# Two attentions and a 64-expert feed forward on one core: down projection four pairs behind the up projection, and a new table of side work

## The reference

```python
shared = silu(xf @ Ws_up) @ Ws_down
aff = xf @ centroids.T
_, idx = top_k(aff + expert_biases, 8)
w = sigmoid(take_along_axis(aff, idx)); w = w / (w.sum() + 1e-8)
cw = zeros((T, 64)).at[arange(T)[:, None], idx].add(w)
h = silu(einsum('td,edf->etf', xf, W_up))
y = einsum('etf,efd->etd', h, W_down)
return shared + einsum('etd,te->td', y, cw)
x = x + attn_a(layernorm(x)); x = x + ffn(layernorm(x))
x = x + attn_b(layernorm(x)); x = x + ffn(layernorm(x))
```

## Time and profile before

| | us |
|---|---|
| median of 3 runs | 1095.35 (1095.05 to 1095.57) |
| the profiled execution | 1094.11 |
| its span in the trace | 1092.0 |
| PE busy | 1001.1 (92%) |
| DVE busy | 956.8 (88%) |
| ACT busy | 890.1 (82%) |
| POOL busy | 487.9 (45%) |

### The profile page before, as it was taken

The page is one execution under the profiler, slowest core; times in us unless marked ns, Lnnn a source line. Parts: engine busy times, 40 slices in busy tenths (PEclk is TensorE's granted clock), DMA queues, the critical chain, the costliest instruction groups (busy, mean ns, idle before and its releaser), DMA issues.

```text
span 1092.0 us, 21659 instructions
## 1 busy us (share of the span) xinstructions
PE 1001.1 (92%) x8016; PEld 513.8 (47%) x8016; DVE 956.8 (88%) x1186; ACT 890.1 (82%) x1466; POOL 487.9 (45%) x893
## 2 busy tenths in 40 slices
PE   6389999999999999999999999999899899999998
PEld 3022222222222222222232337777777777777876
DVE  7799999999999999999999948787877987687665
ACT  5179999999999999999999986777776776677775
POOL 3363545454545555554456466433224332432431
PEclk9579999999999999999999999999999999999999
DMA  8911110111011101110110017665577476757773
GB/s 278 303 33 46 52 50 4 50 51 51 3 51 51 51 4 51 51 34 20 51 51 22 2 27 192 152 163 135 143 175 176 134 172 167 192 145 176 187 192 101
DMA packets 80472, 108.90 MB, mean 100 GB/s; under 512 B 23536, under 2 KB 33520, under 8 KB 80368
## 3 DMA queue, kind: packets, MB, share of 16 engines
q1 hardware_dynamic: 66336, 100.98, 35.1%
q10 hardware_dynamic: 14032, 6.55, 2.3%
HBM read 95.57 MB, written 11.93 MB: 98 GB/s over the span
## 4 chain that ended last, share of the span: by engine, by line
DVE 51%; PE 29%; ACT 7%; issue 5%; DMA 4%; POOL 2%; ACTq 1%; SPq 1%; DVEq 0%; POOLq 0%
DVE NEGMAX L1060 43%; PE PS L1451 8%; PE PS L1453 7%; PE PS L1452 7%; DVE HL L1109 2%; PE PS L1353 2%; ACT HH L943 2%; DVE HF L1101 2%; ACT PR L855 2%; DMA RAWU<-in_L_ffn_W_up_dram 2%; PE PS L1326 1%; PE PS L1232 1%; ACT L950 1%; POOL WUL L627 1%; DMA GATE<-gate_d 1%
## 5 line engine op out<-in xcount | busy, mean ns | idle before, releaser
L1060 DVE TENSOR_REDUCE NEGMAX<-PS 128x1 f32<-128x1024 f32 x512 | 584.5, 1208 | 9.9 <-PE PS L1289 9.2
L855 ACT ACTIVATE PR<-PS 128x512 f32<-128x512 f32 x1024 | 538.7, 600 | 36.5 <-PE PS L1326 24.2
L1353 PE MATMUL PS<-PR,VG 128*32 128x256 f32 (+1 forms) x3840 | 321.2, 406 | 17.5 <-ACT PR L855 2.0
L1326 PE MATMUL PS<-QB,KB 32*128 32x512 bf16 x1024 | 260.1, 387 | 3.0 <-DMA QB<-shift_d 1.7
L1289 PE MATMUL PS<-KA,QA 32*128 32x512 bf16 x1024 | 204.4, 397 | 30.9 <-DVE NEGMAX L1060 22.5
L1101 DVE TENSOR_TENSOR HF<-PS,GATE 128x1024 f32<-128x1024 f32 x128 | 156.2, 1221 | 73.8 <-ACT PS L950 72.0
L950 ACT ACTIVATE PS<-PS 128x1024 f32<-128x1024 f32 x128 | 129.3, 1010 | 93.5 <-PE PS L1453 93.1
L1326 PEld LDWEIGHTS PS<-QB,KB 32*128 32x128 bf16 x1024 | 75.0, 91 | 239.2 <-ACT PR L855 138.1
L943 ACT ACTIVATE HH<-HF 128x1024 fp32r<-128x1024 f32 (+1 forms) x136 | 139.7, 1028 | 19.5 <-DVE HF L1101 18.7
L1109 DVE TENSOR_TENSOR HL<-HF,HH 128x1024 fp32r<-128x1024 f32 (+1 forms) x104 | 129.8, 1248 | 12.5 <-ACT HH L943 12.5
L767 POOL TENSOR_TENSOR HL<-HF,HH 128x1024 fp32r<-128x1024 f32 (+1 forms) x32 | 70.2, 2194 | 155.0 <-ACT HH L943 155.0
(11 more groups left out here) (186 smaller groups left out, 970.6 us busy)
## 6 DMA issues: line engine op xcount, KB each, us to landing
GATE<-gate_d SPq DMA_DIRECT2D x256, 256.0 KB, 4.1
QA<-q_stack SPq DMA_DIRECT2D x64, 128.0 KB, 2.6
QB<-q_stack SPq DMA_DIRECT2D x16, 256.0 KB, 3.0
KB<-k_stack SPq DMA_DIRECT2D x16, 256.0 KB, 3.0
KA<-k_stack SPq DMA_DIRECT2D x60, 64.0 KB, 2.4
q_stack<-PARTS SPq DMA_DIRECT2D x12, 256.0 KB, 4.3
k_stack<-PARTS SPq DMA_DIRECT2D x12, 256.0 KB, 4.4
RAWU<-in_L_ffn_W_up_dram ACTq DMA_DIRECT2D x4, 512.0 KB, 11.9
```

Of the source, the lines that this page charges most:

```text
L855: nc.scalar.activation(PR[:, s % PRING, r, :], PS[:, SCORE_BANK[n], :], ACT.Exp, scale=SCALE_A).then_inc(p_ready, 1)
L1060: nc.vector.tensor_reduce(NEGMAX[:, hs % 2, col:col + 1], PS[:, e:e + 2, :].rearrange("p b n -> p (b n)"), axis=AX_X, op=ALU.max, negate=T ...
L1326: mm(PS[:, SCORE_BANK[n], :], KB[strip, u, mt * P:(mt + 1) * P], QB[strip, u, half * BANK:(half + 1) * BANK], start=True, stop=True).then_ ...
L1353: last = mm(PS[STRIP * r:STRIP * (r + 1), 7, cols], VG[:, u, mt, r // 2, :], PR[:, s % PRING, r, cols], start=mt == 0, stop=mt == TB - 1 a ...
```

## The change

- `LAG` goes from 3 to 4: `down` runs four pairs behind `up`. HH and HL have five places; HF keeps four, under a number of its own (`FPLACES`).
- ACT copies AFF out at the beginning of the step of its `affinity`, with the other side work, and no longer behind silu and `high`. The sigmoid alone stays at the step's end.
- `CWT`, `GRAM`, `GK` and `VMIX` have one copy, not two; POOL's `sum` waits for the `gate_T` before it, and the sigmoid waits for the `sum` before it.
- The table is written anew from chunk 2 on. Routing of chunk 3 moves from (2, 1), (2, 3), (2, 5), (2, 7) to (2, 4), (2, 6), (2, 7), (2, 8) for `affinity`, `top`, `sum`, `gate_T`. That of chunk 5 moves from (3, 16), (4, 1), (4, 3), (4, 5) to (3, 14), (3, 16), (4, 1), (4, 3), and that of chunk 7 likewise in chunks 5 and 6. The second attention's items in chunks 2 and 4 come one step later, up to `mix_back` at (3, 3) and (5, 3). `out_b` stays at (3, 5), (3, 6), (5, 5) and (5, 6).
- 32 `low` stay on POOL; (2, 8), (3, 3), (4, 8) and (5, 3) go to DVE, (1, 16), (2, 2), (4, 2) and (6, 2) come to POOL.

```diff
-LAG = 3
+LAG = 4
+FPLACES = 4
 HPLACES = LAG + 1
...
-    (2, 0): [("x_T", ("f", 3))], (2, 1): [("affinity", 3)], (2, 3): [("top", 3)], (2, 5): [("sum", 3)], (2, 7): [("gate_T", 3)],
+    (2, 1): [("x_T", ("f", 3))], (2, 4): [("affinity", 3)], (2, 6): [("top", 3)], (2, 7): [("sum", 3)], (2, 8): [("gate_T", 3)],
...
-        HF = sb("HF", [P, HPLACES, 2, BANK])
+        HF = sb("HF", [P, FPLACES, 2, BANK])
...
                         pool.wait_ge(wrec_ok, arg + 1)
+                        if arg:
+                            pool.wait_ge(*evacuated(("gate_T", arg - 1)))
...
-                    if routing != (stage == "affinity" and item not in TAIL_SIDE):
+                    if routing and (stage != "affinity" or item in TAIL_SIDE):
                         continue
...
                     elif stage == "affinity":
-                        side_evac(item, AFF, PS[:, bank, 0:4 * E].rearrange("p (t e) -> p t e", e=E))
+                        if not routing:
+                            side_evac(item, AFF, PS[:, bank, 0:4 * E].rearrange("p (t e) -> p t e", e=E))
+                            continue
                         act.wait_ge(*evacuated(item))
+                        act.wait_ge(ch_ok, arg)
                         nc.scalar.activation(EX, AFF, ACT.Sigmoid).then_inc(ex_ok, 1)
                     elif stage == "gate_T":
-                        if arg >= 2:
-                            act.wait_ge(gate_w, 16 * (arg - 1))
-                        side_evac(item, CWT[:, arg % 2, :], PS[0:E, bank, :])
+                        act.wait_ge(gate_w, 16 * arg)
+                        side_evac(item, CWT[:], PS[0:E, bank, :])
...
-                h, k, z = full_before(g), g % HPLACES, 2 * (g % ZSLOTS)
+                h, k, z = full_before(g), g % FPLACES, 2 * (g % ZSLOTS)
                 dve.wait_ge(silu_ok, g + 1)
                 dve.wait_ge(gate_ld[h % GSLOTS], 32 * (h // GSLOTS + 1))
-                if g >= HPLACES:
-                    dve.wait_ge(hh_ok, g - HPLACES + 1)
+                if g >= FPLACES:
+                    dve.wait_ge(hh_ok, g - FPLACES + 1)
```

More of the change, by code:

```diff
@@ L164 @@
     (1, 13): [("sum", 2)], (1, 14): [("norm", ("f", 3))], (1, 15): [("gate_T", 2)],
-    (2, 0): [("x_T", ("f", 3))], (2, 1): [("affinity", 3)], (2, 3): [("top", 3)], (2, 5): [("sum", 3)], (2, 7): [("gate_T", 3)],
-    (4, 1): [("top", 5)], (4, 3): [("sum", 5)], (4, 5): [("gate_T", 5)],
-    (6, 1): [("top", 7)], (6, 3): [("sum", 7)], (6, 5): [("gate_T", 7)], (6, 7): [("y_T", 5)],
+    (2, 1): [("x_T", ("f", 3))], (2, 4): [("affinity", 3)], (2, 6): [("top", 3)], (2, 7): [("sum", 3)], (2, 8): [("gate_T", 3)],
+    (4, 1): [("sum", 5)], (4, 3): [("gate_T", 5)],
+    (6, 1): [("sum", 7)], (6, 3): [("gate_T", 7)], (6, 7): [("y_T", 5)],
     (7, 5): [("y_T", 6)],
@@ L179 @@
     c, f = 2 * b + 1, 2 * b + NCH
[L180 to L193, removed]
+    also((n, 5), ("y_T", n - 1), ("stats", ("b", c)))
+    also((n, 7), ("norm", ("b", c)))
+    also((n, 9), ("x_T", ("b", c)))
+    also((n, 10), ("gram", b))
+    also((n, 11), ("gram_k", b))
+    also((n, 12), ("q_k", b))
+    also((n, 13), ("energy", b))
+    also((n, 14), ("soft_exp", b), ("soft_mix", b))
+    also((n, 15), ("mix_T", b))
+    also((n, 16), ("v_mix", b))
+    also((n + 1, 0), ("v_all", 2 * b))
+    also((n + 1, 1), ("v_all", 2 * b + 1), ("mix_out", b))
+    also((n + 1, 3), ("mix_back", b))
     also((n + 1, 5), ("out_b", 2 * b), ("stats", ("f", f)))
     also((n + 1, 6), ("out_b", 2 * b + 1), ("stats", ("f", f + 1)))
-    also((n + 1, 7), ("norm", ("f", f)))
+    also((n + 1, 7), ("y_T", n), ("norm", ("f", f)))
     also((n + 1, 8), ("norm", ("f", f + 1)))
@@ L208 @@
     also((n + 1, 13), ("sum", f))
+    also((n + 1, 14), ("affinity", f + 1))
     also((n + 1, 15), ("gate_T", f))
-    also((n + 1, 16), ("affinity", f + 1))
+    also((n + 1, 16), ("top", f + 1))
 def full_before(g):
@@ L561, in write_gates @@
                 sp.wait_ge(*evacuated(("gate_T", n)))
-                sp.dma_start(gate_d[n], CWT[:, n % 2, :]).then_inc(gate_w, 16)
+                sp.dma_start(gate_d[n], CWT[:]).then_inc(gate_w, 16)
             write_gates(0)
@@ L765, in low @@
                     pool.wait_ge(down_ok, g - HPLACES + 1)
[L766 to L767 removed]
+                k, f, u = g % HPLACES, g % FPLACES, 2 if is_full(g) else 1
+                nc.gpsimd.tensor_tensor(HL[:, k, 0:u, :], HF[:, f, 0:u, :], HH[:, k, 0:u, :].bitcast(F32),
                                         op=ALU.subtract).then_inc(hl_pool, 1)
@@ L941, in high @@
                     act.wait_ge(silu_ok, g + 1)
-                k, u = g % HPLACES, 2 if is_full(g) else 1
-                nc.scalar.activation(HH[:, k, 0:u, :], HF[:, k, 0:u, :], ACT.Copy).then_inc(hh_ok, 1)
+                k, f, u = g % HPLACES, g % FPLACES, 2 if is_full(g) else 1
+                nc.scalar.activation(HH[:, k, 0:u, :], HF[:, f, 0:u, :], ACT.Copy).then_inc(hh_ok, 1)
             def silu(g):
@@ L951, in silu @@
                     return
-                if g >= HPLACES:
[L953 to L956, removed]
+                if g >= FPLACES:
+                    act.wait_ge(hh_ok, g - FPLACES + 1)
+                    act.wait_ge(hl_ok, lows_before(g - FPLACES + 1, False))
+                    act.wait_ge(hl_pool, lows_before(g - FPLACES + 1, True))
+                nc.scalar.activation(HF[:, g % FPLACES, 0, :], PS[:, z, :], ACT.Silu).then_inc(silu_ok, 1)
             def chunk_sum(n):
@@ L1107, in low @@
                 dve.wait_ge(hh_ok, g + 1)
-                k, u = g % HPLACES, 2 if is_full(g) else 1
-                nc.vector.tensor_tensor(HL[:, k, 0:u, :], HF[:, k, 0:u, :], HH[:, k, 0:u, :].bitcast(F32),
+                k, f, u = g % HPLACES, g % FPLACES, 2 if is_full(g) else 1
+                nc.vector.tensor_tensor(HL[:, k, 0:u, :], HF[:, f, 0:u, :], HH[:, k, 0:u, :].bitcast(F32),
                                         op=ALU.subtract).then_inc(hl_ok, 1)
@@ L1424, in side @@
                         pe.wait_ge(*evacuated(("gram", arg)))
-                        last = mm(PS[:, bank, 0:DIM], GRAM[:, arg, :], WB[:, 1, :], start=True, stop=True)
+                        last = mm(PS[:, bank, 0:DIM], GRAM[:], WB[:, 1, :], start=True, stop=True)
                     elif stage == "q_k":
                         pe.wait_ge(*evacuated(("gram_k", arg)))
-                        last = mm(PS[:, bank, 0:DIM], WB[:, 0, :], GK[:, arg, :], start=True, stop=True)
+                        last = mm(PS[:, bank, 0:DIM], WB[:, 0, :], GK[:], start=True, stop=True)
                     elif stage == "energy":
@@ L1442, in side @@
                         pe.wait_ge(*evacuated(("x_T", ("b", arg))))
-                        last = chunk(VMIX[:, arg // 2, :], arg)(bank)
+                        last = chunk(VMIX[:], arg)(bank)
                     elif stage == "out_b":
```

20 lines of the change are left out of this document (10 added, 10 removed).

## The result

| | before | after |
|---|---|---|
| median, us | 1095.35 (1094.93 to 1095.63, 5 runs) | 1090.65 (1088.37 to 1092.31, 5 runs) |
| ratio | | 0.9954, interval 0.9941 to 0.9967 |
| the profiled execution | 1094.11 | 1090.65 |
| its span | 1092.0 | 1088.8 |

The change is faster: by 4.7 us between the medians, by 0.46% by the ratio. Forecast were 6.8 us. The two profiled executions differ by 3.5, their spans by 3.2.

A forecast was written before the change was run, and what follows sets the result against it. PE was taken as the bound in quiet stretches, with DVE nearly full where routing stands. Removed 22 us, less 14.3 of new waits and 1.35 for the clock, gave 6.4, taken as 6.8: 1088.5 us, range 1082 to 1093.

The forecast's parts named there:

- Halves, 10.5: PE's waits on HH and HL, 8.7 us idle in nine waits; their removal was counted as 10.5 us.
- YS, 5.7: PE's waits on YS, 7.8 us idle; 5.7 us would be removed, five waits of about 0.47 left.
- AFF, 3.7: Three PE waits behind AFF's copy, 3.2 us idle, 3.7 in starts, would go with the copy ahead of silu.
- (2, 8), 4.2: PE would wait 4.2 us at `gate_T` of chunk 3, the worst place, with 1.35 us for a clock drop.
- (1, 15), (3, 15), (5, 15), 2.8 + 2.4 + 1.7 = 6.9: New PE waits at `gate_T` of chunks 2, 4 and 6: 2.8, 2.4 and 1.7 us.
- Chunk 0, 3.1: 3.1 us of waits remain there, on `norm` ahead of `x_T` at (0, 8) and on `gate_T` at (0, 15).
- "What costs nothing", RT: RT lands 5.1 us after its issue, `out_b` comes after 6.5 to 7; without that cover 1 to 3 us, twice.
- 0.4 that I added for rounding: Added to the gain of 6.4 us for the carry of rounding over a hundred steps, giving 6.8.
- The waits only change place: Rival, 11 in 100: PE's removed waits return at `x_T` and `gate_T` in the same stretch; 1095.1 us.
- More is won: Rival, 12 in 100: side chains keep up and the four `gate_T` waits don't come, 1076 us; half of them, 1082.
- Slower: Rival, 7 in 100: four `gate_T` waits are longer behind other POOL or DVE work; 2.5 us more each gives 1098.5.
- The drain of about 1380 ns: Possible extra per table switch on ACT: sigmoid holds ACT 5.7 us, the (2, 8) wait is 6.9, time some 1091.

The follow-up runs named there:

- e4: The change with AFF's copy back behind silu and `high`, ahead of the sigmoid: 1096.95 us, ratio 1.0029 to the kernel of before.
- e7: The change with chunk 0's `x_T`, `affinity` and `top` one step later, and one `low` moved from POOL to DVE: 1092.52 us, ratio 0.9966.
- e1: The change with the table of before and the old place of AFF's copy, so LAG 4 and places alone: 1096.72 us, ratio 1.0029.
- e5: The change itself run once more, as the yardstick for kernels beside it: 1090.41 us, ratio 0.9957.
- e3: The change with `gate_T` of chunk 3 at (2, 10) and not (2, 8): 1088.63 us, ratio 0.9954.
- e8: The change with chunk 0's routing one step later and `gate_T` of chunk 3 at (2, 10): 1087.00 us, ratio 0.9929.
- e6: The change with `out_b` multiplying XT in place of RT, PE waiting for RT's DMAs only four steps later: 1088.81 us, ratio 0.9937.
- e10: e8 with `gate_T` moved from step 15 to step 16 in chunks 0, 1, 3 and 5: 1102.47 us, ratio 1.0078.

## Why the prediction was right, and where its sizes were off

The direction, the mechanism and most sizes held. By its own steps, idle times plus 0.16 a wait:

- **Halves, 10.5:** one wait of 0.4 is left, at (4, 1), on the POOL `low` of (3, 14) that I had at 0.1. Right but for half a microsecond: 10.0.
- **YS, 5.7:** 7.8 in seven waits became 2.5 in five: 5.3 + 2 x 0.16 = 5.6. Right, and five of about half a microsecond are left, as forecast.
- **AFF, 3.7:** gone, 3.7. As the price of the edit this was the largest miss: e4 is 6 to 8 us slower, 3.5 of them seen in its trace, where with LAG 4 the waits behind the copy are 10.3 us and no longer 3.2. The sum isn't touched, for it counted only what was there before.
- **(2, 8), 4.2:** 4.00 + 0.16 = 4.16, with the clock drop that I gave it. Adding up the engines' queues row by row gave this to the first decimal, and not by luck: counted from 771.53, where `up(2, 4)` ends, the silu behind the sigmoid ends at 6.2 (forecast 6.2), `top` at 10.5 (10.4), `sum` at 13.5 (13.6) and POOL's CH at 14.2 (14.4 with its signals).
- **(1, 15), (3, 15), (5, 15), 2.8 + 2.4 + 1.7 = 6.9:** 1.64 + 1.68 + 1.38 and 0.48, 5.2. Too high by 1.7; why these are shorter stays open.
- **Chunk 0, 3.1:** 2.42 + 0.86 + 0.32 = 3.6. But I spread it over two places and gave no clock drop to it: 1.4 more. In e7 the idle time is the same in two pieces, and no drop follows.
- **"What costs nothing", RT:** the step that failed. I set the 5.1 of the read the earlier trace rows against 6.5 to 7 us from its issue to `out_b`. That distance is the one of before less one step (835.33 - 825.62 - 2.78 = 6.9), and so it silently takes the write ahead of the read at what it lasted there, 3.8 us; the read is issued only when the write has landed. The row of before, and then the issues of the change on ACT's queue:

```profile
mixed_d<-VP ACTq DMA_DIRECT2D x2, 512.0 KB, 3.8
```

```profile
822.51 0.39 ACTq L932 DMA_DIRECT2D mixed_d<-VP  x1
828.34 0.35 ACTq L937 DMA_DIRECT2D RT<-mixed_d  x1
```

```profile
mixed_d<-VP ACTq DMA_DIRECT2D x1, 512.0 KB, 5.8
RT<-mixed_d ACTq DMA_DIRECT2D x1, 512.0 KB, 5.6
```

The second is issued 828.34 - 822.51 = 5.83 after the first, when the write has landed: 2.0 us later than the forecast had it. From there PE is at `out_b` after 4.7 us, not 6.5 to 7, and the read takes 5.6. The round trip is 11.4 us from 822.51, and PE is at `out_b` 10.5 us behind it; with a write of 3.8 RT would have been in time. In all traces the write lands after 3.8 to 3.9 us where it stands at (3, 0) and (5, 0) (before, e1), and after 4.7 to 6.0 one step later. The mean DMA share during the first write is 0.65 before and 0.90 with the change; whether that traffic is the cause wasn't tested. The text priced the loss of this cover at 1 to 3 us each; single waits of 1.05, 1.3, 2.51 and 2.88 are in the traces of the change, e5, e3 and e7, and none in those of e4 and e8. The five runs without it (e6) lie within 1.4 us, those of e5 within 3.5.

The sum with the measured sizes: removed 10.0 + 5.6 + 3.7 + 0.8 + 1.4 = 21.5. Come: 4.2 + 5.2 + 3.6 + 1.2 (RT) + 0.5 (an `affinity` at (3, 14), 0.3 idle) + 2 x 1.4 for the clock = 17.5. That leaves 4.0, where the spans differ by 3.2; I took 6.8. Against the 6.4 of the sum that is 2.4 less: 1.2 for RT, 1.4 for the second clock drop, 0.5 each for the halves, for chunk 0 and for `affinity`, and 1.7 back at the three `gate_T`. The 0.4 that I added for rounding had no ground. The 0.8 between 4.0 and the spans stays unassigned. The median moved by 4.7, the two profiled executions by 3.5, and the five runs of the change lie within 3.9 us, so a term of half a microsecond can't be told from the noise in the times; it is read from the traces alone.

**The rivals.** *The waits only change place* is true of the idle time in chunk 0 (e7) and of most of it behind (2, 8) (e3), but not of the clock drops, and not of the sum: DVE's lateness is carried on, while what came from ACT's order, YS and AFF, was won. *More is won* fell: the `gate_T` waits came. *Slower* had its mechanism in the trace, with a small price. At (3, 15):

```profile
865.85 1.30 POOL L760 TENSOR_TENSOR X<-X,BO 128x512 f32<-128x512 f32 x1
...
866.13 2.11 DVE L1114 TENSOR_TENSOR HL<-HF,HH 128x1024 fp32r<-128x1024 f32 x1
```

A `low` of 1.21 us lasts 2.11 while POOL adds two SBUF operands: 0.9 us ahead of the `gate_T` that then waits 1.68; that it is 0.9 us of this wait is argued from the queue, no run took it away. It is also no price of the change: in the kernel of before the `low` at 867.00 lasts 2.08, with the same add of POOL at 866.73. The Trainium skill (SBUF — State Buffer, Who interferes with whom) says that a DVE instruction with two SBUF inputs contends with a GpSimd instruction that reads SBUF, and calls the port pair that they share an exclusive lock. The row agrees, since 865.85 + 1.30 + 1.2 is 868.35 and `low` ended at 868.24. I had allowed up to 2.4 at each of four places; it is 0.9 at one.

The table loads cost what the row said: in e10's rows the sigmoid starts 0.01 behind its load (871.96 + 1.28 against 873.25), and silu 0.01 behind the second. The drain of about 1380 ns that the Trainium skill (ScalarE: Activation LUTs, What ACT_TABLE_LOAD costs) adds to each switch isn't there, nor is the 6.9 us wait at (2, 8) that would follow from it: 4.00 was measured.

## What to carry to other kernels

A deeper pipeline can move the waits from the pipelined work to the side work that shares its engines: e1 is slower than before though every wait on a half is gone. So retime the table with the depth, and put whatever frees a shared bank ahead of operations that wait for the late engine. Add up each engine's queue by rows before moving an item, ACT's copies included: the misses at e4 and e10 came from leaving ACT's queue out. The miss at RT came from carrying a DMA's landing time over to another step. And where a table also steers something else, as it does the choice of the `low` for POOL here, look at what an edit of it moves besides.
